# Modulation matmuls with high and low weights side by side in one stationary tile, halves summed by VectorE

## The reference, cut to what matters

```python
h1 = gelu(einsum('btc,hc->bth', x, Wn1) + bn1)          # 256 -> 64 channels
mod = 0.5 + sigmoid(einsum('bth,dh->btd', h1, Wn2) + bn2)  # 64 -> 8
traces = vmap(lambda tau, m: causal_ema(gated * m[..., None], tau))(tau_raws, moveaxis(mod, -1, 0))
```

## Time and profile before

| | us |
|---|---|
| median of 3 runs | 1045.18 |
| lowest and highest | 1044.25 and 1045.28 |
| span of the profiled execution | 1044.1 |
| TensorE busy in it | 1036.7 |
| VectorE busy | 756.8 |
| ScalarE busy | 405.0 |
| GpSimd busy | 16.3 |

### The profile page before, as it was taken

How to read it: one execution, slowest core, us unless ns; L and a number is a source line. 1 busy time by engine, 2 the same in 40 slices (tenths; PEclk the granted TensorE clock), 3 DMA queues, 4 the chain that set the end, 5 groups by cost and what they waited for, 6 DMA issues and landing times.

```text
span 1044.1 us, 12751 instructions
## 1 busy us (share of the span) xinstructions
PE 1036.7 (99%) x4850; PEld 861.1 (82%) x4850; DVE 756.8 (72%) x1260; ACT 405.0 (39%) x663; POOL 16.3 (2%) x26
## 2 busy tenths in 40 slices
PE   8999999999999999999999999999999999999998
PEld 5688888888888888888888888888888888888898
DVE  6989977799547986389764996559955599545236
ACT  8654555423443234422344223433334432423232
POOL 1200000000000000000000000000000000000000
PEclk9999999999999999999999999999999999999999
DMA  5388999786354754466544664546645465355582
GB/s 213 121 313 275 312 356 356 282 324 240 131 192 167 257 181 162 162 238 210 197 164 163 231 235 152 185 162 242 208 154 201 163 235 204 146 201 191 203 323 90
DMA packets 38302, 223.02 MB, mean 214 GB/s; under 512 B 4514, under 2 KB 5282, under 8 KB 16610
## 3 DMA queue, kind: packets, MB, share of 16 engines
q1 hardware_dynamic: 35938, 209.63, 56.1%
q0 software_dynamic: 2304, 12.58, 3.2%
HBM read 188.51 MB, written 33.69 MB: 213 GB/s over the span
## 4 chain that ended last, share of the span: by engine, by line
PE 96%; DMA 2%; DVE 2%; issue 0%; SPq 0%; ACT 0%; DVEq 0%
PE ps_up L665 14%; PE ps_up L695 14%; PE ps_up L696 14%; PE ps_down L737 14%; PE ps_down L741 14%; PE ps_down L738 14%; PE ps_aux L658 2%; PE ps_aux L659 2%; PE ps_aux L660 2%; DMA wi<-split_wi 1%; DVE y L1633 1%; PE ps_aux L837 1%; PE ps_aux L834 1%; PE ps_aux L833 1%; PE ps_aux L822 1%; PE ps_aux L818 1%
## 5 line engine op out<-in xcount | busy, mean ns | idle before, releaser
L1065 ACT ACTIVATE hid_hi<-ps_up 128x512 fp32r<-128x512 f32 (+1 forms) x336 | 193.5, 576 | 507.8 <-PE ps_up L665 507.6
L1306 DVE SCALAR_TENSOR_TENSOR hid_lo<-ps_up,hid_hi 128x512 fp32r<-128x512 f32 (+1 forms) x336 | 220.1, 658 | 228.9 <-ACT hid_hi L1065 227.5
L695 PE MATMUL ps_up<-x_hi_all,wi 128*128 128x512 f32 (+1 forms) x660 | 250.8, 382 | 0.4 <-DMA wi<-split_wi 0.4
L696 PE MATMUL ps_up<-x_hi_all,wi 128*128 128x512 f32 (+1 forms) x660 | 249.9, 380 | 0.0
L737 PE MATMUL ps_down<-hid_hi,wo 128*128 128x512 f32 (+1 forms) x640 | 245.3, 384 | 0.1
L738 PE MATMUL ps_down<-hid_hi,wo 128*128 128x512 f32 (+1 forms) x640 | 245.1, 384 | 0.0
L665 PE MATMUL ps_up<-x_lo_all,wi 128*128 128x512 f32 (+1 forms) x660 | 197.4, 380 | 0.2 <-DVE x_lo_all L1297 0.2
L741 PE MATMUL ps_down<-hid_lo,wo 128*128 128x512 f32 (+1 forms) x640 | 193.9, 384 | 0.0
L695 PEld LDWEIGHTS ps_up<-x_hi_all,wi 128*128 128x128 f32 x660 | 124.1, 188 | 24.1 <-DMA wi<-split_wi 0.8
L696 PEld LDWEIGHTS ps_up<-x_hi_all,wi 128*128 128x128 f32 x660 | 124.1, 188 | 23.0
L665 PEld LDWEIGHTS ps_up<-x_lo_all,wi 128*128 128x128 f32 x660 | 122.0, 188 | 24.3 <-DVE x_lo_all L1297 0.4
(11 more groups left out here) (248 smaller groups left out, 855.1 us busy)
## 6 DMA issues: line engine op xcount, KB each, us to landing
wi<-split_wi SPq DMA_DIRECT2D x70, 1024.0 KB, 4.8
wo<-split_wo SPq DMA_DIRECT2D x70, 1024.0 KB, 4.9
modb<-mod_scratch SPq DMA_DIRECT2D x28, 512.0 KB, 4.6
split_wi<-wi SPq DMA_DIRECT2D x10, 1024.0 KB, 7.3
split_wo<-wo SPq DMA_DIRECT2D x10, 1024.0 KB, 7.6
xt<-in_x SPq DMA_DIRECT2D x8, 512.0 KB, 5.8
split_wi<-ex POOLq DMA_DIRECT2D x4, 1024.0 KB, 8.6
split_wo<-ex POOLq DMA_DIRECT2D x4, 1024.0 KB, 6.0
```

Of the source, the lines that this page charges most:

```text
L695: pe.matmul(ps, w_hi, x2_hi[:, parity, c, tokens], start=c == 0, stop=False)
L696: pe.matmul(ps, w_lo, x2_hi[:, parity, c, tokens], start=False, stop=False)
L1065: act.activation(hid_hi[:, k % NU, tokens], ps_up[k % NU][:, tokens], ACT.Relu).then_inc(hid_hi_ready, 1)
L1306: dve.scalar_tensor_tensor(hid_lo[:, k % NU, tokens], ps_up[k % NU][:, tokens], 0.0, f32(hid_hi[:, k % NU, tokens]), ALU.max, ALU.subtract ...
```

## The change

Both stationary tiles of the modulation get the high weights and the low weights side by side, in different columns, instead of three products (or two) that are summed in PSUM. The columns of the stationary tile become partitions of the result: for mod_hidden the high product is on partitions 0 to 63 and the low product on 64 to 127; for mod they are on partitions 0 to 7 and 32 to 39. mod_hidden takes four matmuls instead of six (the tile by x high and x low, for two channel halves). For mod, modh_hi and modh_lo lie one above the other in a single 128-partition tile, modh_parts, so that one matmul takes both instead of two. The low weights by the low data are thereby in the sum too.

The two halves have to be added. ScalarE copies the low half out of PSUM (mod_hidden_low, mod_low), VectorE adds the high half from PSUM (mod_hidden_sum, mod_sum) and by that frees the bank; Gelu and sigmoid then read from SBUF. The plans move accordingly:

| step | engine | slot before | slot after |
|---|---|---|---|
| mod_hidden_low (new) | ScalarE | | 1 |
| mod_hidden_sum (new) | VectorE | | 1.5 |
| mod_hidden (Gelu, high part) | ScalarE | 1 | 2, ahead of soma |
| mod_hidden_lo | VectorE | 1.5 | 2.5 |
| mod | TensorE | 2.5, ahead of gate_hidden | 3, behind gate_hidden |
| mod_low (new) | ScalarE | | 3.5 |
| mod_sum (new) | VectorE | | 3.5, behind gate_logits |
| mod (sigmoid, plus 0.5) | ScalarE | 3 | 4.5, ahead of gate_exp |
| mod (store) | SyncE | 3 | 4 |
| modb0, modb1 | SyncE | 4 | 5 |

In period 0 mod_low is at ScalarE slot 0.5, mod_sum at VectorE slot 0.5 and mod at ScalarE slot 1. In the opening VectorE prepares the low columns. The core of the diff:

```diff
 PLAN_TENSOR = {
-    0.5: ["mod_hidden"], 1.5: ["soma"], 2.5: ["mod", "gate_hidden"], 4.5: ["wgate"],
+    0.5: ["mod_hidden"], 1.5: ["soma"], 2.5: ["gate_hidden"], 3: ["mod"], 4.5: ["wgate"],
...
 PLAN_SCALAR = {
-    1: ["mod_hidden", "gate_part_hi"], 2: ["soma"], 3: ["mod"], 4: ["gate_exp"], 5.5: ["wgate"],
+    1: ["mod_hidden_low", "gate_part_hi"], 2: ["mod_hidden", "soma"], 3.5: ["mod_low"], 4.5: ["mod", "gate_exp"], 5.5: ["wgate"],
...
 PLAN_VECTOR = {
-    0.5: ["gate_part"], 1.5: ["mod_hidden_lo"], 2: ["gate_part_lo"], 3.5: ["gate_logits"],
+    0.5: ["gate_part"], 1.5: ["mod_hidden_sum"], 2: ["gate_part_lo"], 2.5: ["mod_hidden_lo"], 3.5: ["gate_logits", "mod_sum"],
...
 PLAN_SYNC = {
-    3: ["mod"], 4: ["modb0", "modb1"], 8: ["store"], 10.5: ["modb2"], 14.5: ["modb3"], 20.5: ["next_x"],
+    4: ["mod"], 5: ["modb0", "modb1"], 8: ["store"], 10.5: ["modb2"], 14.5: ["modb3"], 20.5: ["next_x"],
...
-    "scalar": {0.5: ["mod"], 2: ["wgate"], 26: ["temp_hi"], 28: ["tgate"], 29: ["sg_hi"],
+    "scalar": {0.5: ["mod_low"], 1: ["mod"], 2: ["wgate"], 26: ["temp_hi"], 28: ["tgate"], 29: ["sg_hi"],
...
-    "vector": {2: ["wgate_scan", "gated"],
+    "vector": {0.5: ["mod_sum"], 2: ["wgate_scan", "gated"],
...
+        modh_hi, modh_lo = modh_parts[0:H1, :], modh_parts[H1:P, :]
+        mod_places = [slice(i * P // 4, i * P // 4 + D) for i in range(2)]
...
-                at = slice(W_N2, W_N2 + P)
-                pe.matmul(ps, wc_hi[:, at], modh_hi[:, :], start=True, stop=False)
-                return pe.matmul(ps, wc_hi[:, at], modh_lo[:, :], start=False, stop=True)
+                return pe.matmul(ps, wc_hi[:, W_N2:W_N2 + P], modh_parts[:, :], start=True, stop=True)
...
-                        mm = product(ps_aux[0][:, :], wc_hi[:, at], wc_lo[:, at], xg_hi[:, c, :], xg_lo[:, c, :],
-                                     c == 0, c == CT - 1)
+                        pe.matmul(ps_aux[0][:, :], wc_hi[:, at], xg_hi[:, c, :], start=c == 0, stop=False)
+                        mm = pe.matmul(ps_aux[0][:, :], wc_hi[:, at], xg_lo[:, c, :], start=False, stop=c == CT - 1)
...
+                elif step == "mod_hidden_low":
+                    act.wait_ge(aux_ready[0], p.aux[0]["mod_hidden"] + 1)
+                    act.activation(modh[0:H1, :], ps_aux[0][H1:P, :], ACT.Copy).then_inc(modh_low, 1)
+                elif step == "mod_low":
+                    act.wait_ge(aux_ready[1], p.aux[1]["mod"] + 1)
+                    act.activation(mod[:, :], ps_aux[1][mod_places[1], :], ACT.Copy).then_inc(mod_low, 1)
                 elif step == "mod_hidden":
-                    act.wait_ge(aux_ready[0], p.aux[0]["mod_hidden"] + 1)
-                    act.activation(modh[:, :], ps_aux[0][:, :], ACT.Gelu, bias=col(C_BN1)).then_inc(aux_free[0], 1)
                     act.wait_ge(aux_free[0], p.aux[0]["mod_hidden"] + 1)
-                    hi(modh_hi[:, :], modh[:, :]).then_inc(modh_hi_ready, 1)
+                    act.activation(modh[0:H1, :], modh[0:H1, :], ACT.Gelu, bias=par[0:H1, C_BN1:C_BN1 + 1])\
+                        .then_inc(modh_ready, 1)
+                    act.wait_ge(modh_ready, n - 1)
+                    hi(modh_hi, modh[0:H1, :]).then_inc(modh_hi_ready, 1)
                 elif step == "mod":
-                    act.wait_ge(aux_ready[1], p.aux[1]["mod"] + 1)
-                    act.activation(mod[:, :], ps_aux[1][0:D, :], ACT.Sigmoid, bias=par[0:D, C_BN2:C_BN2 + 1])\
-                        .then_inc(aux_free[1], 1)
                     act.wait_ge(aux_free[1], p.aux[1]["mod"] + 1)
+                    act.activation(mod[:, :], mod[:, :], ACT.Sigmoid, bias=par[0:D, C_BN2:C_BN2 + 1]).then_inc(mod_sig, 1)
+                    act.wait_ge(mod_sig, n)
                     act.activation(mod[:, :], mod[:, :], ACT.Copy, bias=0.5).then_inc(mod_ready, 1)
...
                 elif step == "mod_hidden_lo":
                     dve.wait_ge(modh_hi_ready, n)
-                    lo(modh_lo[:, :], modh[:, :], modh_hi[:, :]).then_inc(modh_split, 1)
+                    lo(modh_lo, modh[0:H1, :], modh_hi).then_inc(modh_split, 1)
+                elif step == "mod_hidden_sum":
+                    dve.wait_ge(modh_low, n - 1)
+                    dve.tensor_tensor(modh[0:H1, :], ps_aux[0][0:H1, :], modh[0:H1, :], ALU.add).then_inc(aux_free[0], 1)
+                elif step == "mod_sum":
+                    dve.wait_ge(mod_low, n)
+                    dve.tensor_tensor(mod[:, :], ps_aux[1][mod_places[0], :], mod[:, :], ALU.add).then_inc(aux_free[1], 1)
...
-                lo(wc_lo[:, 0:W_N2], raw_wc[:, 0:W_N2], wc_hi[:, 0:W_N2])
-
-                at = slice(W_N2, W_N2 + P)
-                lo(wc_hi[H1:P, at], raw_wc[H1:P, at], wc_hi[H1:P, at]).then_inc(wc_ready[0], 1)
+                step(lo(wc_lo[:, 0:W_N2], raw_wc[:, 0:W_N2], wc_hi[:, 0:W_N2]))
+                low_half = [t[:, 0:W_N2].rearrange("p (c h) -> p c h", c=CT)[:, :, H1:P] for t in (wc_hi, raw_wc)]
+                sync()
+                lo(low_half[0], low_half[1], low_half[0])
+                low_mod = slice(W_N2 + mod_places[1].start, W_N2 + mod_places[1].stop)
+                lo(wc_hi[:, low_mod], raw_wc[:, low_mod], wc_hi[:, low_mod]).then_inc(wc_ready[0], 1)
```

## The result

The changed kernel takes 1055.19 us (median of four runs, 1054.56 to 1056.83) against 1045.03 of the kernel before (median of four as well): ratio 1.0098, with a 95% interval of 1.0084 to 1.0112. It is 1% slower, although 19 matmuls are gone from the bound engine. The profiled execution has a span of 1055.2 us, 11.1 more than before.

The account below looks back on a forecast made before the run. TensorE was taken as the bound, busy 99% of the span at 0.2267 us per matmul. -4.31 + 8.0 + 3.85 + 1.1 + 0.1 = +8.7 us gave span 1052.8, time 1053.9 us; range 1049.5 to 1057.5.

Parts of the forecast that it names:

- Removal (section 1): TensorE, mod_hidden and mod: 19 matmuls fewer at 0.2267 us each, 4.31 us less.
- Soma's wait (section 2): Slot 1.5, six periods: TensorE waits for mod_hidden_sum behind relu_lo(3), chain 2.27 against 1.36, 0.91 us each.
- The sign that was announced: TensorE idle before soma 0.8 to 0.9 us and before mod about 0.6, six times each, 1.1 longer in b = 1.
- Mod's wait (section 3): Slot 3, six periods: TensorE waits for mod_hidden_lo, which stands behind relu_lo(4) on VectorE, 0.68 us each.
- the split starts 0.61 later: In mod's chain on VectorE: mod_hidden_lo's split starts 0.61 us after relu_lo(4) starts.
- b = 1, two tile splits more: Expert tile splits on VectorE behind relu_lo(3) and relu_lo(4) lengthen both waits by 1.13 each: 3.85 us.
- b = 0 (section 4): First period: the sigmoid waits for mod_sum, relu(3) starts 3 us late; 0.9 + 0.23 = 1.1 us of waiting.
- The rest (section 5): Opening's extra split and wait, 0.1 us (0 to 0.3); late mod steps, copies, store and modb loads cost nothing.
- The cover: Slots 3.5 to 5: VectorE's 0.92 us wait at slot 5's second scan hides the late mod steps; failing, below 1 us.
- (a): Rival: the waits are hidden and only the matmul removal counts, 1040.9 us; 7%.
- (b): Rival: only one wait occurs, 1048.7 us without mod's or 1047.3 without soma's; 9%.
- (c): Rival: late mod steps hurt further, 1 to 3 us in b = 0, up to 0.3 in six periods: 1055.5 to 1058.5; 12%.

Follow-up runs that it names:

- e9: The changed kernel run again, nothing edited: 1054.45 us, ratio 1.009.
- e5: The kernel before with the 19 matmuls left out (part of the product missing), all waits and steps unchanged: 1042.14 us, ratio 0.9964.
- e1: The changed kernel with mod_hidden_sum moved on VectorE from slot 1.5 to 1, ahead of relu_lo(3): 1047.98 us, ratio 1.0027.
- e7: The changed kernel with modh_lo in its own tile on partitions 0 to 63, mod's matmul taking only modh_hi's 64 rows: 1057.61 us, ratio 1.0107.
- e10: The version of e4 run again with more rounds: 1040.59 us, ratio 0.9962.
- e3: The changed kernel with both mod_hidden_sum and mod_hidden_lo moved earlier on VectorE, ahead of relu_lo(3) and relu_lo(4): 1042.13 us, ratio 0.9967.
- e2: The changed kernel with mod_hidden_lo moved on VectorE from slot 2.5 to 2, ahead of relu_lo(4): 1048.73 us, ratio 1.0031.
- e4: As e3, and in period 0 ScalarE's sigmoid and copy of mod moved from slot 1 to 1.5, behind relu(3): 1040.88 us, ratio 0.9958.
- e8: The kernel before with the mod steps, store and modb loads as late as in the change: 1045.07 us, ratio 1.0002.
- e6: The changed kernel with b = 1's two expert tile splits moved on VectorE from k = 1 and 2 to 0 and 3: 1053.85 us, ratio 1.0082.

## Why the prediction was right, point by point

The forecast was 1053.9 us and slower. Measured were 1055.19, and 1054.45 in e9. The mechanism was the one forecast; some sizes were off.

**Removal (section 1), -4.31.** Right: e5's distances give -4.32. The Trainium skill's 131 ns per 512-column matmul ("TensorE: Matmul & The Clock Gate", section "Back-to-back issue gap") would have made it -2.5; the runs don't agree, at 227 ns.

**Soma's wait (section 2), 0.91.** Right to the hundredth in b = 3, and each step of the chain as read: down at 439.69, relu at 439.89, hid_lo at 440.52, the sum at 441.13, soma at 441.85. The sum, of which before had no row, took 0.67 where 0.68 was taken. Removing it alone (e1) gives it back in each period (1.06 to 1.13 falls to 0.08 to 0.11, a little more than 0.91). The sign that was announced, idle time of 0.8 to 0.9 us in front of soma and 0.6 in front of mod, came at the right places with smaller numbers, 0.64 and 0.54, since the idle time leaves 0.27 of each wait out.

**Mod's wait (section 3), 0.68.** Mis-sized: 0.81. Of the 0.13, 0.11 is the term "the split starts 0.61 later", which was 0.72. The earlier trace rows gave 0.61 for a split whose output begins on partition 0; in the change it goes to partitions 64 to 127, and e7, which puts it back on 0, has 0.61 again, in all five periods b = 2 to 6. In b = 1 it is 1.24 instead of 1.13. A rule of the Trainium skill that I had not weighed ("VectorE: DVE Perf Modes", section "Two Vector instructions with no wait between them") states this: an instruction whose output starts in another quadrant, a group of 32 partitions, than the last one in that memory starts only when the earlier ones have finished. The trace agrees: 446.91 plus 0.69 is 447.60, and the split starts at 447.63. The split of the change also writes on other partitions than it reads; the runs don't tell this apart from the change against the instruction ahead.

**b = 1, two tile splits more, 3.85.** Measured 2.05 + 1.91 = 3.96, of which 0.1 is the term just named. What was not foreseen is the half clock, 1.65 us in the first profiled execution. The prediction counted no time for the clock, because the earlier trace rows show full clock through the idle stretches of the opening. That was too quick a reading: a row of tenths over 40 slices shows no such stretch, as the clock row of the kernel after is also 9 throughout. The kernel before did have full clock, 1.00 from 5 to 1030 us, but that says nothing of the new idle stretches in the middle of a period.

**b = 0 (section 4), 1.1.** Right in size, 0.87 net against 0.9, and along the chain: relu(3) at 63.18 (63.15 predicted), the second gate sigmoid at 69.05 (69.0), relu(5) at 71.11 (71.15), and VectorE 0.85 late (0.9). Half right in place: it was to appear in front of L741, down's matmul with hid_lo. Some 0.3 us does, at 106.14 and 109.06 (L746 in the kernel after). Most of it appears at 110.19 in front of up, where TensorE meets a split of the raw wi from the same late VectorE. I had looked only at the hid_lo at 132.81 and not at the other things that TensorE takes from VectorE on the way.

**The rest (section 5).** The cover held. VectorE of the kernel after, b = 3:

```profile
459.15 2.33 DVE L1416 TENSOR_TENSOR_SCAN gates<-alpha,ps_aux 128x512 f32<-128x512 f32 x2
...
468.83 1.41 DVE L1465 SCALAR_TENSOR_TENSOR temporal<-modb,blend_w,gates 128x512 f32<-128x512 f32 x2
```

The 0.92 us of idle time at the second scan are gone, TensorE waits for nothing there, and modb is read without a wait. The opening came out 0.05 us shorter in the profiled execution, within its scatter.

**From span to time.** I took 1.1 us for the time outside the span by setting the profiled span against the median. In the runs where both are known it is 1.6 (1056.83 and 1055.2; 1039.99 and 1038.4 in e10). The profiled execution of before was thus a run of about 1045.7, not a median one. The predicted span of 1052.8 is within 0.1 of e9's 1052.9, but that closeness is partly luck: e9's periods cost 9.5 us where 8.6 were predicted, and its opening was 0.7 shorter than before's. Of the 0.9, 0.65 is mod's wait (five times 0.13). Another 0.03 to 0.06 per period lies right behind soma's wait: from its second matmul to the first of up, eleven steps, it is 2.49 us in the kernel before, in e1 and in e3, where soma does not wait, and 2.52 to 2.55 in every later period of the kernel after, e9 and e2, where it does.

**Rivals.** (a), hidden waits and 1040.9, describes the version of e4 and e10 (1040.88 and 1040.59), not the change as planned. (b), one wait alone, at 1047.3 or 1048.7, is what e1 and e2 made on purpose: 1047.98 and 1048.73. (c) fell for the later periods with e8; in b = 0 the distance, 0.87 against 0.9, leaves nothing for it.

**Open.** Only the profiled execution of a kernel shows the half clock itself; for the others a mean clock of 0.998 and a span that is longer by about 2 us stand for it. By that, behind the same soma wait of b = 1, it came in one of four runs of the kernel after, in none of four in e9, none of four in e6, none of six in e2, and in three of four in e7. One of eight runs of e1, which has no soma wait but a mod wait of 1.7 us of idle time in b = 1, has these signs too. The two profiles that show it have one more thing in common: the transfer of an expert tile landed late just then. In the kernel after,

```profile
184.81 1.06 ACT L1030 ACTIVATE ex<-ex 128x1024 fp32r<-128x1024 f32 x1 [2.09 <-DMA ex<-in_expert_wo]
```

and 2.54 us in e7, while ScalarE did not wait for that tile in e9 and e2. Whether that plays a part, and what decides in an execution, was not found.

## What to carry to other kernels

Fewer instructions on the bound engine are worth their spacing only if the steps that feed it are still in time. For each new step, note what stands ahead of it in its engine's order and when that can end, and compare with when the bound engine gets there; here a 1.36-us gap had to hold a chain of 2.27 us. If the feeding engine is idle just ahead of that place, the step often can go one slot earlier for nothing: three entries of the plans turned +9 to +10 us into -4.5 us. And look for the first place at which a late engine is met among all the things it delivers, not among one kind.

## What the runs showed of the hardware that I had not expected

- A VectorE instruction that writes from partition 64 on, behind one that writes from partition 0 on, started only when that one had ended: 0.72 us after its start instead of 0.61, and 1.24 instead of 1.13 behind one of 1024 columns.
- A matmul of 64 rows between matmuls of 128 rows was followed by the next after 0.43 us, behind a wait and without one; one of 128 rows in the same place was followed after 0.34 behind a wait and after 0.23 without.
- 1.3 us after 1.8 us of idle time had ended, TensorE's granted clock went to 0.51 (the 1.2 GHz level) from 186.50 to 189.90 in one profile of the changed kernel and stayed at 1.00 in the other; it cost 1.65 us.
- The idle time that the profile gives for a wait of TensorE is 0.27 us below what the wait costs by the start times (0.64 and 0.91; 0.54 and 0.81).
